# Sixteen pipeline steps instead of four in the body of a loop that five engines run

## The chip, the cores and the metric

The kernel runs on one core of a Trainium2 chip, as one launch. The metric is the device time of that launch in microseconds (us); lower is better. A core has five engines, each with an instruction stream of its own: TensorE (PE; its weight loads are shown apart as PEld), VectorE (DVE), ScalarE (ACT), GpSimd (POOL) and SyncE (SP), which here only issues DMAs. They meet at semaphores.

## The reference

Four batches of 1024 tokens with 128 features. First an attention block with a residual and a layer norm, then six local layers on its result, then one more residual and layer norm. The local layers are nearly all of the work:

```
for i in range(DEPTH):                       # 6 layers
    x = attn_layer(shift_tokens(x), Wqkv[i], q_scale[i], k_scale[i], Wo[i]) + x
    x = ffn_layer(shift_tokens(x), ln_g[i], ln_b[i], W1[i], b1[i], W2[i], b2[i]) + x

attn_layer: q, k, v = split(x @ Wqkv)        # 16 heads of 64
            q, k = l2norm(q) * qs, l2norm(k) * ks, both rotated by tables of position
            softmax over windows of 32 queries against 64 keys, times v, then @ Wo
ffn_layer:  layer norm, @ W1 -> a, gate (341 each);  (a * gelu(gate)) @ W2
```

## The kernel before

`build` makes four parts that follow each other, with all engines meeting between them: `clear_first_rows`, `mla_attention` (the first block; it has a loop of its own over batches, which is not touched), `local_layers`, and `closing_norm`.

`local_layers` cuts a layer into 16 pairs of token tiles (4 batches of 4 pairs, 256 tokens each). The six layers are thus 96 pairs, and the engines run 96 steps plus three that drain the pipeline. A step works on four pairs at different stages: it projects q, k and v for pair t, does scores, softmax and the product with v for pair t-1, the output projection for pair t-2 and the feed-forward part for pair t-3. Each engine's order in a step is written out by hand, and every step has the same order. Four steps (`POS`) are one batch of one layer, which the code calls a round; there are 24 rounds (`ROUNDS`), so 6 layers of 4 rounds.

Every engine's program is made by `rounds(eng, step_fn)`: the first round is written out, with numbers in its semaphore waits, then a hardware loop over rounds 1 to 23 has one round of four steps as its body, with the waits' values worked out in registers from the loop's counter, and then come the three draining steps. In the loop the Python objects `Step` and `Pair` turn the counter into those values, `s.p` is the step's place in its round (0 to 3), and what happens only at some places (SP reloads the projection weights at `s.p == 3`; VectorE and GpSimd clear their link semaphore there) is decided when the program is made. These weights are reloaded in every round, also where the layer stays the same.

On TensorE a step is, in this order: transposes of q and k (L457) with projections (L411) between them, the scores (L468 and L476, two halves for each of two groups of windows), the transpose of the normed x (L498), the product with Wo (L490, `times_wo`), the feed-forward matmuls (L510) among transposes of the probabilities (L421) and projections of v (L411), the transpose of the next x (L397), the product with v in two halves (L433 and L443, `times_v`) around early projections for the next pair (L411), the last feed-forward matmul (L518), one more projection (L411) and the transpose of its result (L498). ScalarE copies each PSUM bank out and frees it; L628 copies the next x once in a step, and L644 the transposed q and k.

Of the kernel before, what the change touches and what calls it, by code (L numbers as in the profile page):

```python
# [22 lines left out]
BATCH, SEQ, DIM = 4, 1024, 128  # L23
# [3 lines left out]
DEPTH, HEADS, DH, WINDOW = 6, 16, 64, 32  # L27
# [5 lines left out]
POS = SEQ // PAIR  # L33
ROUNDS = DEPTH * BATCH
# [100 lines left out]
def local_layers(nc, x_dram, x1_dram, w):  # L135
# [5 lines left out]
    with ExitStack() as ctx:  # L141
# [96 lines left out]
        def rounds(eng, step_fn, last_fn=None):  # L238

            for p in range(POS):
                step_fn(Step(0, p))
            with eng.Fori(1, ROUNDS) as f:
                for p in range(POS):
                    step_fn(Step(f, p))
            for t in range(PAIRS, PAIRS + MAX_LAG):
                step_fn(Step(ROUNDS, t - PAIRS))

# [27 lines left out]
        def _(sp):  # L276
# [40 lines left out]
            def step(s):  # L317
# [47 lines left out]
                if runs(back3):  # L365
# [3 lines left out]
                    if s.p == 2 and in_rounds(s):  # L369

                        load_ffn(s.f)

            rounds(sp, step)
            sp.wait_ge(x2_out, 16 * PAIRS)

        @block.tensor
        def _(pe):
# [148 lines left out]
            def step(s):  # L527
# [60 lines left out]
                if runs(back3):  # L588
                    pe.wait_ge(a_free, ring_a.at(s, "y2T")[1] + 1)
                    transpose_pair(s, "y2", lambda a: y2T[:, P * a:P * (a + 1)])  # L590

            rounds(pe, step)

        @block.scalar
        def _(act):
# [128 lines left out]
            for i in range(EARLY):  # L725
                square(Step(-1, POS - 1).pair(-1), i)
            rounds(act, step)

# [1022 lines left out]
```

## Time and profile before

| what | value |
|---|---|
| median of 3 runs (lowest, highest) | 4710.56 us (4701.91, 4711.07) |
| profiled execution: its own time | 4716.59 us |
| its span, first to last instruction | 4714.8 us |
| PE / PEld busy | 4147.4 (88%) / 2777.6 (59%) us |
| DVE / ACT / POOL busy | 2916.1 (62%) / 2622.4 (56%) / 2799.6 (59%) us |
| mean granted TensorE clock | 0.957 |
| instruction packets: queue q8, queue q14 | 581 (9.52 MB), 147 (1.20 MB) |

The span has three stages: up to about 915 us the first attention block, to about 4680 us the 99 steps of the local layers, then the closing norm. Busy time is the union of an engine's instructions; idle time is put down to what ended it ("<-").
### The profile page before, as it was taken

The page shows a single profiled execution, that of the slowest core. Times are in us where ns is not written, and L with a number is a line of the kernel's source. Part 1 is how long each engine was busy: PE and PEld are TensorE (multiplying, and loading weights), DVE is VectorE, ACT ScalarE, POOL GpSimd, SP SyncE. Part 2 cuts the span into 40 slices and gives each one's busy share as a digit, 9 for nine tenths or more (in the row PEclk, how much of TensorE's full clock was granted, in tenths as well). Part 3 has the DMA queues.
Part 4 walks back from the last instruction along what each step waited for, and adds up shares of the span by engine and source line. Part 5 has one row for each costly group of instructions (what it writes and reads, how often), then busy time and mean ns, then how long its engine had stood idle before and what let it go on. Part 6 is the DMA issues. An engine that isn't in the chain of part 4 may idle for free. (4 is left out here: it accounts for less than half of the span.)

```text
span 4714.8 us, 163642 instructions
## 1 busy us (share of the span) xinstructions
PE 4147.4 (88%) x67078; PEld 2777.6 (59%) x67078; DVE 2916.1 (62%) x4217; ACT 2622.4 (56%) x4417; POOL 2799.6 (59%) x3584
## 2 busy tenths in 40 slices
PE   5878788689999999999999999999999999999994
PEld 2434344356666666666666666666666666666663
DVE  5565656566666666666666666666666666666664
ACT  2535354446556565665656655656566555665662
POOL 0000000177777777777777777777777777777771
PEclk9979788899999999999999999999999999999997
DMA  0000000112222122222222222222222222222223
GB/s 27 3 15 2 16 16 3 42 45 58 69 71 72 51 69 65 72 57 64 65 69 64 56 66 69 77 53 69 65 72 56 65 65 69 64 56 65 69 66 79
DMA packets 284548, 258.85 MB, mean 55 GB/s; under 512 B 122872, under 2 KB 258509, under 8 KB 271149
## 3 DMA queue, kind: packets, MB, share of 16 engines
q1 hardware_dynamic: 283820, 248.14, 19.7%
q8 instruction: 581, 9.52, 0.9%
q14 instruction: 147, 1.20, 0.1%
HBM read 117.63 MB, written 29.77 MB: 31 GB/s over the span
## 5 line engine op out<-in xcount | busy, mean ns | idle before, releaser
L785 DVE TENSOR_TENSOR products<-bank_d,table 128x1024 f32<-128x1024 f32 x772 | 938.1, 1216 | 716.5 <-ACT sq L612 711.8
L908 POOL TENSOR_TENSOR products<-products 128x2048 f32<-128x2048 f32 x192 | 870.4, 4533 | 263.1 <-DVE products L785 263.1
L411 PE MATMUL bank_d<-w_qkv,xT 128*128 128x512 f32 x1544 | 805.6, 625 | 25.2 <-DVE products L785 14.2
L612 ACT ACTIVATE sq<-bank_d 128x512 f32<-128x512 f32 x772 | 467.8, 606 | 484.8 <-PE bank_d L411 474.6
L945 POOL TENSOR_TENSOR qk_rot<-products,rnorm 128x2048 f32<-128x2048 f32 x192 | 695.4, 3622 | 15.0 <-POOL rnorm L927 14.6
L783 DVE TENSOR_REDUCE ss<-sq 128x16 f32<-128x1024 f32 x386 | 468.7, 1214 | 240.3 <-ACT sq L612 240.3
L952 POOL TENSOR_TENSOR prob<-prob,inv_sum 128x1024 f32<-128x1024 f32 x192 | 365.1, 1902 | 407.3 <-DVE inv_sum L765 407.3
L872 POOL MEMSET ident<- 128x128 f32 x1 | 0.2, 204 | 914.6 <-POOLq L1062 914.6
L1489 DVE TENSOR_REDUCE part_max<-s_max 128x1 f32<-128x512 f32 (+3 forms) x768 | 398.3, 554 | 150.7 <-PE s_max L1238 101.2
L457 PE MATMUL bank_a<-ident,qk_rot 128*128 128x128 f32 x3072 | 412.6, 290 | 69.6 <-issue 64.0
L457 PEld LDWEIGHTS bank_a<-ident,qk_rot 128*128 128x128 f32 x3072 | 366.9, 149 | 150.4 <-issue 103.0
L411 PE MATMUL bank_a<-w_qkv,xT 128*128 128x512 f32 x768 | 403.0, 607 | 43.7 <-ACT gate L667 40.5
L1410 ACT ACTIVATE a_probT<-s_T 128x1024 f32<-128x1024 f32 x320 | 299.1, 938 | 249.0 <-PE s_T L1253 152.1
L476 PE MATMUL scores<-kT,qT 64*32 64x64 f32 x24576 | 427.5, 218 | 8.9 <-issue 8.9
L476 PEld LDWEIGHTS scores<-kT,qT 64*32 64x32 f32 x24576 | 362.8, 107 | 99.9 <-issue 99.0
L659 ACT ACTIVATE attnT<-bank_a 128x512 f32<-128x512 f32 x384 | 208.5, 595 | 341.7 <-PE bank_a L443 341.7
L443 PE MATMUL bank_a<-probT,v_back 64*64 64x32 f32 x12288 | 380.2, 221 | 0.0
L443 PE MATMUL bank_a<-probT,v 64*64 64x32 f32 x12288 | 376.6, 220 | 2.6 <-issue 2.1
L648 ACT ACTIVATE prob<-prob 128x1024 f32<-128x1024 f32 x192 | 203.0, 1057 | 284.8 <-DVE prob L755 283.8
L443 PEld LDWEIGHTS bank_a<-probT,v_back 64*64 64x64 f32 x12288 | 332.6, 135 | 42.2 <-issue 40.8
L764 DVE TENSOR_REDUCE row_sum<-prob 128x16 f32<-128x1024 f32 x192 | 233.2, 1215 | 197.7 <-ACT prob L648 197.7
L490 PE MATMUL bank_a<-attnT,w_o 128*128 128x256 f32 x1536 | 350.9, 382 | 1.5 <-issue 1.5
(168 smaller groups left out, 7551.9 us busy)
## 6 DMA issues: line engine op xcount, KB each, us to landing
v_back<-v SPq DMA_DIRECT2D x96, 768.0 KB, 5.5
w_qkv<-in_Wqkv_dram SPq DMA_DIRECT2D x25, 1024.0 KB, 5.0
v_back<-v SPq DMA_DIRECT2D x192, 128.0 KB, 5.5
w_qkv<-in_Wqkv_dram SPq DMA_DIRECT2D x25, 512.0 KB, 5.5
xs<-x_layers SPq DMA_DIRECT2D x194, 64.0 KB, 2.1
w_o<-in_Wo_dram SPq DMA_DIRECT2D x24, 512.0 KB, 6.0
xr<-x_layers SPq DMA_DIRECT2D x96, 128.0 KB, 2.2
x<-x SPq DMA_DIRECT2D x96, 128.0 KB, 1.8
```

The lines of the kernel that those rows point to most:

```text
L411: nc.tensor.matmul(bank[:, :], xT[:, P * a:P * (a + 1)], w_qkv[:, col:col + 512], start=True, stop=True).then_inc(d_filled if i < 8 else a ...
L443: last = nc.tensor.matmul(banks[u][64 * h2:64 * h2 + 64, col:col + 32], src[64 * u:64 * u + 64, a, DH * h:DH * (h + 1)], probT[ph][64 * u: ...
L457: last = nc.tensor.transpose(bank[:, P * j:P * (j + 1)], qk_rot[:, a, col:col + P], ident[:, :])
L476: last = nc.tensor.matmul(scores[row:row + 32, hp, u, :], qT[64 * h2:64 * h2 + 64, hp, 32 * win:32 * win + 32], kT[pair.par][64 * h2:64 * ...
L490: last = nc.tensor.matmul(bank[:, 0:PAIR], w_o[:, hp, :], attnT[:, hp, :], start=(hp == 0), stop=(hp == HP - 1))
L612: nc.scalar.activation(sq[j % 2][:, 8 * c:8 * c + 8, :], bank_d[slot][:, :].rearrange("p (h d) -> p h d", d=DH), ACT.Square).then_inc(squa ...
L783: nc.vector.tensor_reduce(ss[:, a, HEADS * kq:HEADS * (kq + 1)], sq[i // 2 % 2][:, :, :], AX.X, ALU.add)
L785: nc.vector.tensor_tensor(products[:, a, head:head + 8, :, :].rearrange("p h r (o d) -> p h r o d", o=2), bank[:, :].rearrange("p (h r d) ...
L908: link(nc.gpsimd.tensor_tensor(products[:, a, :, 0, :], products[:, a, :, 0, :], products[:, a, :, 1, :], ALU.add))
L945: nc.gpsimd.tensor_tensor(qk_rot[:, a, :].rearrange("p (h d) -> p h d", d=DH), products[:, a, :, 0, :], rnorm[:, a, 0:2 * HEADS].unsqueeze ...
L952: nc.gpsimd.tensor_tensor(prob[ph][:, :, :], prob[ph][:, :, :], inv_sum[:, ph, :].unsqueeze(2).to_broadcast([P, HEADS, 2 * WINDOW]), ALU.m ...
L1489: nc.vector.tensor_reduce(part_max[:, head, col:col + 1], s_max[m % 2][:, 0:width], AX.X, ALU.max).then_inc(max_free, 1)
```

## The change

`rounds` writes out the first four rounds (one layer, 16 steps) instead of one, and its loop runs over layers 1 to 5 with the 16 steps of a layer as its body. The steps themselves, their order, the waits, the DMAs and the draining steps are what they were. In the loop a wait's value is now worked out from the layer's counter.

```
         def rounds(eng, step_fn, last_fn=None):
-            for p in range(POS):
-                step_fn(Step(0, p))
-            with eng.Fori(1, ROUNDS) as f:
+            for b in range(BATCH):
                 for p in range(POS):
-                    step_fn(Step(f, p))
+                    step_fn(Step(b, p))
+            with eng.Fori(1, DEPTH) as layer:
+                for b in range(BATCH):
+                    for p in range(POS):
+                        step_fn(Step(BATCH * layer + b, p))
             for t in range(PAIRS, PAIRS + MAX_LAG):
                 step_fn(Step(ROUNDS, t - PAIRS))
```

The changed file has two lines more, so a line number above 243 is larger by two in it. TensorE before, at the end of the loop's body: the last projection and transpose of a round, the branch, and behind the loop the first matmuls of the draining steps.

```order
L518 MATMUL bank_a<-gate,w 128x256 x3
L382 REGISTER_ALU
L411 MATMUL bank_d<-w_qkv,xT 128x512
L589 REGISTER_ALU
L382 REGISTER_ALU
L498 MATMUL bank_d<-ident,y2T 128x128 x2
L243 REGISTER_ALU
L243 COMPARE_AND_BRANCH
```

TensorE of the changed kernel at the end of a round that is inside the new body: the next round's first transposes (L459) follow with no branch between.

```order
L520 MATMUL bank_a<-gate,w 128x256 x3
L384 REGISTER_ALU
L413 MATMUL bank_d<-w_qkv,xT 128x512
L591 REGISTER_ALU
L384 REGISTER_ALU
L500 MATMUL bank_d<-ident,y2T 128x128 x2
L455 ISA
L391 ISA
L459 MATMUL bank_a<-ident,qk_rot 128x128 x4
```

The branch is gone from three of four round ends inside the body; it stays, as `L244 COMPARE_AND_BRANCH`, at the end of a layer.

TensorE of the changed kernel at the end of the first round (written out): here before stood `L243 UNCONDITIONAL_BRANCH`, the entry into the loop, and then the loop's first transposes with a `REGISTER_ALU` ahead of each group of four.

```order
L520 MATMUL bank_a<-gate,w 128x256 x3
L413 MATMUL bank_d<-w_qkv,xT 128x512
L500 MATMUL bank_d<-ident,y2T 128x128 x2
L459 MATMUL bank_a<-ident,qk_rot 128x128 x16
L413 MATMUL bank_d<-w_qkv,xT 128x512
L459 MATMUL bank_a<-ident,qk_rot 128x128 x16
L413 MATMUL bank_d<-w_qkv,xT 128x512
L470 MATMUL scores<-mask,ident_b 128x512
```

## Rows read from the trace of the kernel before

**Rows 1.** The page, busy time and slices

```profile
PE 4147.4 (88%) x67078; PEld 2777.6 (59%) x67078; DVE 2916.1 (62%) x4217; ACT 2622.4 (56%) x4417; POOL 2799.6 (59%) x3584
PEclk9979788899999999999999999999999999999997
```

**Rows 2.** Waits of PEld from 1071 to 4604 us: total, times, longest us

```profile
PEld scores L468 <- ACT kT L644: 102.7, 92, 1.1
...
PEld bank_a L457 <- issue: 100.4, 121, 3.8
...
PEld bank_a L411 <- ACT gate L667: 78.8, 92, 1.0
...
PEld bank_a L421 <- ACT yT L694: 49.5, 62, 0.8
...
PEld bank_a L490 <- issue: 32.1, 23, 1.6
...
PEld bank_d L411 <- DVE products L785: 14.3, 11, 1.9
```

**Rows 3.** Timeline of ACT, start and length in us, the copy L628

```profile
1064.14 0.38 ACT L628 ACTIVATE xT<-bank_a 128x256 f32<-128x256 f32 x1
...
1101.59 0.38 ACT L628 ACTIVATE xT<-bank_a 128x256 f32<-128x256 f32 x1
...
1138.40 0.38 ACT L628 ACTIVATE xT<-bank_a 128x256 f32<-128x256 f32 x1
...
1175.19 0.38 ACT L628 ACTIVATE xT<-bank_a 128x256 f32<-128x256 f32 x1
...
1212.49 0.38 ACT L628 ACTIVATE xT<-bank_a 128x256 f32<-128x256 f32 x1
...
1255.47 0.38 ACT L628 ACTIVATE xT<-bank_a 128x256 f32<-128x256 f32 x1
...
4594.50 0.38 ACT L628 ACTIVATE xT<-bank_a 128x256 f32<-128x256 f32 x1
```

**Rows 4.** Line 243 (the loop) by engine: ns min/median/max, first and last start

```profile
L243 PEldq COMPARE_BRANCH  x23: 83/3665/3896, 1222.1 to 4603.9; - x23
...
L243 DVEq COMPARE_BRANCH  x23: 50/56/74, 1224.0 to 4605.4; - x23
...
L243 POOLq COMPARE_BRANCH  x23: 40/45/45, 1217.9 to 4599.9; - x23
```

**Rows 5.** Timeline of PE at a taken branch (1376.9) and the last (4603.9)

```profile
1376.53 1.77 PE L411 MATMUL bank_d<-w_qkv,xT 128*128 128x512 f32 x2 [1.91 <-issue]
...
1380.97 2.39 PE L457 MATMUL bank_a<-ident,qk_rot 128*128 128x128 f32 x10 [2.24 <-issue]
...
4603.28 1.12 PE L411 MATMUL bank_d<-w_qkv,xT 128*128 128x512 f32 x2 [0.18 <-issue]
...
4604.46 1.73 PE L457 MATMUL bank_a<-ident,qk_rot 128*128 128x128 f32 x14
```

**Rows 6.** Windows: length, busy PE PEld DVE ACT POOL, clock, DMA, GB/s

```profile
1376.87:1383.70 6.83, 4.59 (x17) 3.19 (x16) 3.33 (x7) 1.79 (x3) 2.30 (x1) 0.50 0.09 27
1383.70:1393.80 10.10, 9.77 (x162) 5.81 (x160) 6.19 (x6) 5.67 (x12) 7.00 (x18) 1.00 0.19 41
```

**Rows 7.** DMA queues from 1226 to 1376 us: packets, MB, share

```profile
q8 instruction: 21, 0.34, 1.0%
q14 instruction: 4, 0.03, 0.1%
```

**Rows 8.** Timeline of PE in the round written out and step 4

```profile
1033.52 0.19 PE L443 MATMUL bank_a<-probT,v 64*64 64x32 f32 x1 [1.92 <-issue]
...
1054.08 2.10 PE L490 MATMUL bank_a<-attnT,w_o 128*128 128x256 f32 x9 [1.49 <-issue]
...
1089.69 0.27 PE L498 MATMUL bank_a<-ident,xn 128*128 128x128 f32 x1 [1.21 <-issue]
```

## The prediction

> **What bounds the kernel now.** I read the page first. TensorE is busy 88% of the span, the next engine 62%, and its granted clock is at 2.4 GHz nearly throughout [rows 1]. The chain that ended last covers only the closing norm, so it does not speak of the loop; the step's length does. ScalarE copies the next x once in a step (L628), so the distance of two such copies is one step [rows 3]: 36.81, 36.79 and 37.30 us, and then 42.98 us, from 1212.49 to 1255.47. That long one holds the loop's branch. The trace has 91 steps from 1101.59 to 4594.50, 3492.91 us in all, with 22 taken branches. If the others take 36.97 (the mean of the three), 129 us are left, 5.9 us for each branch; if they take 36.8, 144 us or 6.5 us. I take **6.2 us for a taken branch**. From 1064.14 to 1101.59 the program passes from the round that is written out into the loop, without a branch and with the same reload of weights, and that step takes 37.45. So the end of a round is not dear; the jump is.
>
> Where do the 6.2 us lie? TensorE's branch instruction takes 3.7 us in the median and 83 ns the one time that it isn't taken [rows 4]. In the shown round TensorE then sits idle 2.24 us ahead of L457; at the last, untaken branch it doesn't [rows 5]. The clock adds to it: 0.50 (1.2 GHz) for 6.83 us around the branch, 1.00 after it [rows 6]. The branch of the other engines takes 45 to 74 ns, and they wait for TensorE meanwhile. A part of the 6.2 us is not the jump: the projection L411 just ahead of it is late too, by 1.91 us in the shown round and 0.18 in the last [rows 5]. I put that at 0.9 us on average, and the jump itself with its slow clock at 5.3.
>
> What is this L411 waiting for? Code arrives in packets of 16 KB, 21 in a time just short of a round [rows 7], for a body of 5,248 instructions: a block is about 256 of them. The two stalls for "issue" in the first round [rows 8] are 768 instructions apart in the program, three blocks exactly, and the third of these rows (1.21 us) five blocks further on. So a **border** between blocks can cost 1 to 2 us where TensorE eats instructions fast (scores, product with v: 256 in about 2 us), since the next block isn't asked for in time. Of some 20 borders in a round most cost nothing. L490 pays in each round (23 times, 32.1 us in all) [rows 2], but two waits behind it, for ScalarE's yT (0.8) and gate (1.0) [rows 2], get shorter by nearly as much: that stall is almost free. A stall between the transpose of the next x and the scores would be paid in full, for there TensorE waits for nothing else.
>
> **The change, part by part.**
>
> *Branches.* 22 taken ones become 4 (five iterations): 18 fewer. With the whole 6.2 us that is 111.6 us. Three round ends of each layer and the three in the first layer turn into plain steps.
>
> *The four that stay.* POOL's body grows from 180 to 714 instructions, VectorE's from 220 to 871, SP's from 97 to 369, so each of them may now have to fetch at the jump as well. POOL's branch of 45 ns [rows 4] may become as long as TensorE's 3.7 us. It comes some 4 us before TensorE's (1217.9 against 1222.1 in the first) and is covered by TensorE's own stall of the same length; without that cover the late one would be qk_rot, at 3.7 us each, 15 us in all. I take 0.
>
> *Borders in the loop.* Before, the body had the same borders in every round, so only the same few places could be unlucky. A step of 1,312 instructions is five blocks and 32 instructions, so over 16 steps the borders drift and pass through every position twice. Placing them by the known stalls (one must lie at L490 of the first step of the old loop and one at its last L411), two in each new iteration fall on the end of the dense product with v or the first L518 behind it, where I expect 2.3 to 2.8 us, paid in full; one falls between the halves of that product, 0.5 to 1.4; two fall on L490, nearly free; the rest on places that cost about nothing in the rows. That makes some 6.5 us per iteration, 32 for five. It takes the place of the 0.9 that each of 22 old round ends paid. Bounds: none at all, and below twice this.
>
> *Borders in the first layer.* A step that is written out has 1,280 instructions, five blocks exactly, so in each of the 12 new steps a border stands in L490 as in the second of [rows 8] (1.49). The two waits behind it give back about 1.3; left are about 0.3 us, 4 in all. If nothing is given back, it is 18.
>
> *Register instructions* of the 12 steps: gone, 32 in a TensorE step. They lie beside running matmuls; plain steps at entry and in the loop differ by less than 1 us. I take 0; if each saved 30 ns it would be 12 us less.
>
> *Sum.* Old excess 22 x 6.2 = 136. New: 4 x 5.3 = 21 for jumps, 32 for borders in the loop, 4 in the first layer, together 57. Gain 79 us. The profiled execution took 4716.6 us, so it would take 4637.6; the median of the runs shown lies 6.0 below it, which gives **4631 us**.
>
> The Trainium skill, "Runtime: NRT & Kernel Launch", section on instruction fetch mechanics, says that the next 16 KiB block (256 instructions) is fetched while the present one runs, that crossing a border is mostly hidden, and that a taken branch out of the window forces a fetch. The trace agrees on the branch (3.7 us) and on most borders, not on all (1.49 and 1.92 us). By the page's rule alone the gain would be the 111.6 us of the branches and no border would cost anything.
>
> **The rivals.**
>
> *Full gain.* Borders cost as little in the new body as in most of the old one, the late L411 vanishes with the branch behind it. For it: only one place in a round of some 20 borders pays regularly, and it is nearly free. Against: the 1.92 in the product with v [rows 8]. 4716.6 - 111.6 - 6.0 = 4599 us. This is what the Trainium skill's rule in the page named above gives.
>
> *Borders bite harder.* Each iteration has four full stalls of 2.5 us instead of two and a half, and two of them pull the clock down as the jump does [rows 6], worth 1.7 more each (of the jump's 5.3, what its 3.7 doesn't explain): 5 x (4 x 2.5 + 2 x 1.7) = 67. The first layer pays 9, half of its bound. With 21 for the jumps that is 97, the gain 39 and the time 4671 us.
>
> *Slower.* One mechanism: asking for the next block late, at most borders. TensorE crosses five borders in each of the 92 steps concerned; the gain of 111.6 is gone when a step loses 1.2 us on average, one border in five at 1.2 us, fully paid. At one in three at 1.25 us (2.1 us a step) the time is 4710.6 - 111.6 + 193 = 4792 us. Against: the plain steps at 36.8 with five borders each [rows 3].
>
> *No change.* The long step is due to the round's end (weights, ScalarE) and not to the jump; then it stays, and the time is 4711 us. Against: 83 ns and no idle time at the untaken branch [rows 4, 5], and 37.45 at the entry [rows 3].
>
> **How the numbers follow.** A measurement of this kernel tells about 0.2% (9.4 us) from no change. Chances: forecast 0.50 (4612 to 4650), full gain 0.25 (4590 to 4612), borders bite harder 0.16 (4650 to 4700), slower 0.05, no change 0.04. The first three are all faster by over 0.2%: so faster 0.91, same 0.04, slower 0.05. The range reaches from a little below the full gain (an excess of 6.5 us instead of 6.2 gives 117 us, 4594) to where harder borders are mostly taken in, 4668.
>
> **What the profile after would show.** TensorE's COMPARE_BRANCH 5 times, four at 3.3 to 3.9 us and one short. Distances of L628 copies of 36.8 to 37.5 at three of four round ends, 42 to 44 at four places only. The clock at 0.50 in the loop four times instead of 22. "issue" ahead of L457 down from 100.4 by about 60 us. New "issue" gaps of 2 to 3 us ahead of L518 or L411 behind the product with v, once in eight steps and always at the same steps; if they are missing, the full gain is right. L490 late in each of the first layer's steps, L421 and L411 waiting less. Wrong would be: round ends that stay at 43 us without a branch, a POOL or VectorE branch of microseconds that TensorE waits for, or plain steps above 38 us throughout.

## The result and the profile after

| | before | after |
|---|---|---|
| median of 4 runs each | 4709.5 us (4701.9 to 4711.1) | 4761.8 us (4757.3 to 4761.9) |
| ratio after / before | | 1.0112, 95% interval 1.0097 to 1.0127 |
| profiled execution | 4716.6 us | 4761.9 us, span 4760.1 |

The changed kernel is **1.1% slower**; 4631 us, 1.7% faster, was predicted. I read its profile in the order of the prediction. The page first: busy time per engine, granted clock in slices, and the queues that carry code (packets, MB).

```profile
PE 4164.5 (87%) x67078; PEld 2787.4 (59%) x67078; DVE 2916.3 (61%) x4217; ACT 2618.1 (55%) x4417; POOL 2805.6 (59%) x3584
PEclk9979888899999999999999999999999999999997
...
q8 instruction: 554, 9.08, 0.8%
q14 instruction: 214, 1.75, 0.1%
```

Nothing there tells where the 52 us between the medians (45.3 between the two profiled executions) went: against [rows 1] TensorE is busy 17 us longer, and the clock's tenths are the same but for one slice. The branches (L244, formerly L243) went as forecast, five times, and none of another engine is long:

```profile
L244 POOLq COMPARE_BRANCH  x5: 40/45/50, 2137.0 to 4645.0; - x5
L244 PEldq COMPARE_BRANCH  x5: 83/3608/3820, 2141.1 to 4648.9; - x5
```

The timeline of ScalarE's copy of the next x, now L630, tells it. The one that ends the first round is at 1065.56 and the 92nd after it at 4639.52, 3574.0 us, against 3530.4 (from 1064.14 to 4594.50) in [rows 3]: 43.6 of the 45.3 us lie in these 92 steps. Round ends without a branch take 36.7 to 37.6 us in the loop, as forecast (one in the first layer takes 38.5). But in each sixteen, steps in the middle are long:

```profile
1693.30 0.38 ACT L630 ACTIVATE xT<-bank_a 128x256 f32<-128x256 f32 x1
...
1735.86 0.38 ACT L630 ACTIVATE xT<-bank_a 128x256 f32<-128x256 f32 x1
...
1780.45 0.38 ACT L630 ACTIVATE xT<-bank_a 128x256 f32<-128x256 f32 x1
...
1817.25 0.38 ACT L630 ACTIVATE xT<-bank_a 128x256 f32<-128x256 f32 x1
...
2006.81 0.38 ACT L630 ACTIVATE xT<-bank_a 128x256 f32<-128x256 f32 x1
...
2048.25 0.38 ACT L630 ACTIVATE xT<-bank_a 128x256 f32<-128x256 f32 x1
...
2093.77 0.38 ACT L630 ACTIVATE xT<-bank_a 128x256 f32<-128x256 f32 x1
```

42.56, 44.59, then 36.80 again; later 41.44 and 45.52. The steps of an iteration are counted from 0, the one that holds the loop's entry or its branch. In the first of the five iterations steps 5, 6, 11, 13 and 14 are such (step 11, not shown, takes 42.4), in the others the same ones, with step 13 between 38.9 and 41.7. The waits of the weight load for "issue" (total, times, longest, us), from 1055 to 4642 us after, and from 1071 to 4604 us before:

```profile
PEld scores L478 <- issue: 118.0, 386, 4.2
PEld bank_a L445 <- issue: 109.5, 122, 5.6
...
PEld bank_a L520 <- issue: 57.9, 165, 3.8
...
PEld bank_a L459 <- issue: 46.7, 112, 4.0
...
PEld bank_a L492 <- issue: 7.9, 9, 1.2
```

```profile
PEld scores L476 <- issue: 95.1, 378, 1.6
...
PEld bank_a L518 <- issue: 44.5, 186, 0.2
...
PEld bank_a L443 <- issue: 39.8, 96, 0.4
```

The jump's wait (L459, before L457) fell from 100.4 [rows 2] to 46.7. The waits of the product with v (L445) grew by 70 us, with single waits of up to 5.6 us; the longest before was 0.4. One of them, in the timeline of TensorE and the windows around it (length, busy PE PEld DVE ACT POOL, clock, DMA share, GB/s):

```profile
1742.16 0.29 PE L445 MATMUL bank_a<-probT,v 64*64 64x32 f32 x6
1747.11 0.31 PE L445 MATMUL bank_a<-probT,v 64*64 64x32 f32 x1 [4.66 <-issue]
```

```profile
1739.00:1742.30 3.30, 3.30 (x115) 2.16 (x113) 1.80 (x2) 2.06 (x4) 2.64 (x8) 1.00 0.90 254
...
1744.84:1751.66 6.82, 4.55 (x25) 3.10 (x26) 1.04 (x1) 1.68 (x3) 1.28 (x2) 0.50 0.09 20
```

A stall of 4.66 us in the middle of a product, and 6.8 us at half the clock (1.2 GHz) that begin 2.3 us before the stall ends. And the DMA engines are 90% busy up to the moment at which TensorE runs dry. The DMA view of 1744.5 to 1745.5 us holds the code packet that ends the stall:

```profile
q1 hardware_dynamic: 65, 0.16, 74.7%
q8 instruction: 1, 0.02, 8.0%
```

From 1739.0 to 1744.5 there is none; it starts at 1744.6, 2.3 us after TensorE ran dry. The late packet I saw at once; the DMA share beside it I read past at first, as the order of the experiments shows.

### The profile page after: what moved, and what is told of

Same layout as the page of the kernel before. It is cut to its first block and busy times, and to the rows that moved or that the text cites. A ratio compares the mean times of both kernels' runs of the same rounds, so it can differ in the third digit from the quotient of the medians.

```text
span 4760.1 us, 162061 instructions
## 1 busy us (share of the span) xinstructions
PE 4164.5 (87%) x67078; PEld 2787.4 (59%) x67078; DVE 2916.3 (61%) x4217; ACT 2618.1 (55%) x4417; POOL 2805.6 (59%) x3584
## 5 line engine op out<-in xcount | busy, mean ns | idle before, releaser
L413 PE MATMUL bank_d<-w_qkv,xT 128*128 128x512 f32 x1544 | 817.1, 633 | 6.2 <-DVE products L787 4.8
L445 PE MATMUL bank_a<-probT,v 64*64 64x32 f32 x12288 | 385.4, 220 | 45.8 <-issue 45.5
L459 PE MATMUL bank_a<-ident,qk_rot 128*128 128x128 f32 x3072 | 390.1, 280 | 20.9 <-issue 14.6
L445 PE MATMUL bank_a<-probT,v_back 64*64 64x32 f32 x12288 | 386.1, 221 | 24.3 <-issue 24.3
L459 PEld LDWEIGHTS bank_a<-ident,qk_rot 128*128 128x128 f32 x3072 | 347.7, 143 | 94.1 <-issue 49.9
L445 PEld LDWEIGHTS bank_a<-probT,v_back 64*64 64x64 f32 x12288 | 335.5, 135 | 69.3 <-issue 67.2
L445 PEld LDWEIGHTS bank_a<-probT,v 64*64 64x64 f32 x12288 | 339.7, 136 | 47.9 <-issue 47.9
```

The lines of the kernel that those rows point to most:

```text
L413: nc.tensor.matmul(bank[:, :], xT[:, P * a:P * (a + 1)], w_qkv[:, col:col + 512], start=True, stop=True).then_inc(d_filled if i < 8 else a ...
L445: last = nc.tensor.matmul(banks[u][64 * h2:64 * h2 + 64, col:col + 32], src[64 * u:64 * u + 64, a, DH * h:DH * (h + 1)], probT[ph][64 * u: ...
L459: last = nc.tensor.transpose(bank[:, P * j:P * (j + 1)], qk_rot[:, a, col:col + P], ident[:, :])
```

## The experiments

Each time is the median of its runs; ratios are to the kernel before on the same chip (4702 to 4712 us). Step times are distances of ScalarE's copy as above. "Theory 1" is the prediction's own, made harsher: a border between code blocks is dear wherever TensorE eats instructions fast.

### Which engine's body costs

TensorE alone gets the body of sixteen, and then all engines but TensorE:

```diff
-            rounds(pe, step)
+            rounds(pe, step, long_body=True)   # other engines: round of four
```

> Only TensorE has the written-out layer and the body of sixteen steps; the other four engines keep the round of four. Theory 1 (borders between TensorE's code blocks): the time is that of the changed kernel, 4762 us within 10, and the slow steps stand at the same places (steps 5, 6, 11, 13 and 14 of each sixteen). Theory 2 (the longer streams of the other engines, whose code packets rose from 147 to 214): clearly below, between 4600 (the gain of 18 branches undisturbed) and 4709.

Measured: 4797.2 us (ratio 1.019, 1.016 to 1.022), its profiled execution 4762.6, the fastest of four that reach up to 4810.5. Each round's end inside the body now takes 38.9, though TensorE doesn't jump there: 18 times 2.1 us is 38, about what the time lies above the 4762 expected (35). Steps 5, 11, 13 and 14 are long again, with the product with v waiting up to 5.6 us at once. But step 6 is long (44.0) in one iteration of the profiled execution only and takes 37.2 to 38.0 in the other four, where the changed kernel has 44 to 45 in all five. TensorE's program is the same in both, so its borders alone do not make this stall.

> The opposite: ScalarE, VectorE, GpSimd and SyncE have the body of sixteen steps, TensorE keeps its round of four. Theory 1: as before, 4709 us within 10. Theory 2: the loss of the changed kernel shows, 4762 us or more, since TensorE keeps its 22 taken branches as well.

Measured: 4707.6 us (0.999, 0.998 to 1.000); round ends at 43. So the loss comes with TensorE's longer code and not with the others', and the round ends of the run before suggest that the other engines' jumps are worth 2.1 us a round where TensorE's own jump doesn't cover them (tested further on).

### Moving all borders

Two kernels were to shift TensorE's code by 128 no-operations. The no-operations were dropped when the program was built, so these are the two kernels of the case once more and say nothing on the theory:

> The kernel before with 128 no-ops on TensorE ahead of its first wait in the local layers, where it idles 22 us anyway; nothing else changes but where the borders between blocks of 256 instructions fall. Theory 1: each of the 23 rounds gets the borders of steps 5 to 8 of the changed kernel's sixteen (42.6, 44.6, 36.8, 36.9 us, 161 in all) and keeps its taken branch (5.3): 166 instead of 153.7 us a round, 23 times, so about 4990 us. Theory 2, or borders that cost little: 4709 to 4716 us.

> The changed kernel with the same 128 no-ops. A step moves the borders by 32 instructions, so 128 are four steps. Theory 1: the slow steps of each iteration move to four places earlier, 1, 2, 7, 9 and 10 instead of 5, 6, 11, 13 and 14; the five iterations take the same within 15 us in all. In the first layer (1,280 instructions a step, borders at fixed places) all borders move by 128, which may cost anything from nothing to 8 us a step: 4762 to 4860 us. Theory 2: the slow steps stay where they are.

Measured: 4708.7 us (0.999, 0.997 to 1.000) and 4766.5 us (1.013, 1.010 to 1.015), a repeat of the result.

What does shift the borders is to place the head of TensorE's loop at a chosen slot of a block of 256. In the kernel before it stands at about 138:

```diff
-            with eng.Fori(1, ROUNDS) as f:
+            loop = nc.Fori(1, ROUNDS, engines=OrderedEngineSet([eng.engine]), head_slot={eng.engine: 10})
+            with loop as f:
```

> The kernel before, with the head of TensorE's loop laid on slot 10 of a block of 256 instructions, where it stands at about slot 138 now. Nothing else changes. Theory 1 (borders): each round gets the borders of steps 5 to 8 of the changed kernel's sixteen (42.6, 44.6, 36.8, 36.9 us) and its taken branch (5.3): 166 instead of 153.7 us a round, about 4990 us. Theory 2 (the losses of the changed kernel come from something else, borders cost little): 4700 to 4720 us.

Measured: **4983.8 us (1.060, 1.054 to 1.065)**. Same instructions, same branches in the loop, 6% slower, within 10 us of what was expected: the first round in the loop reads 43.4, 44.7, 37.1, 42.6. The borders' places matter more here (274 us) than all branches together (about 145).

> The same with the head on slot 66, so that the four steps get the borders of the changed kernel's steps 7 to 10, which took 36.7 to 36.9 us nearly always. Theory 1: the late last projection of a round (0.9 us) goes, the taken branches stay: 0.9 x 22 = 20 us less than before, 4690 us. Theory 2: 4700 to 4720 us.

Measured: 4788.6 us (1.018, 1.016 to 1.020). Missed by 100 us: in the fourth step of 22 of the 23 rounds TensorE waits 3.0 to 4.1 us at a border in the scores, although step 10 of the changed kernel, which has its borders at the same places, took 36.7. Carrying step times over from the changed kernel named the dear places at slot 10 and failed here, so the place of a border does not by itself give its price.

### Announcing the branch

Rival (the announced branch does not help, only the place of borders matters): 4700 to 4710. Second rival (some border stalls by 3.5 us a round as with slot 66): 4700 or more, one step of each round at 40 to 41.

> The same as the run with slot 106, and the back branches of the other engines' loops announced too (their heads stay where they are). If the 39 us that remain at each round's end are the other engines' jumps (2.1 us a round by the run in which PE alone had no branch), the round end falls from 39.1 to 37 to 38: 4570 to 4600 us. Rival: the others' branches stand too near a block's beginning for the announcement to help, or their blocks are hidden anyway: the same as slot 106 alone, within 0.2%.

Measured: 4718.1 us (1.002, 1.000 to 1.003); 4745.2 (1.008, 1.005 to 1.010); 4723.0 (1.005, 1.003 to 1.007); 4694.6 (0.998, 0.997 to 1.000). Expected were 4620, 4600, 4613 and 4570 to 4600: all four missed, the first because the announcement does nothing at the old place, the others because of stalls at borders that are left. TensorE's branch in the first two, by line (the 24th in the second is the entry into the placed loop):

```profile
L248 PEldq COMPARE_BRANCH  x23: 88/3666/3866, 1216.6 to 4606.9; - x23
```

```profile
L248 PEldq COMPARE_BRANCH  x24: 87/456/1487, 1070.0 to 4633.1; - x24
```

With the hint at the old place, where the branch stands some 10 instructions behind a border (138 + 5,248 is 21 blocks and 10), it still takes 3.7 us; where it stands 190 or more behind one, 0.5 us. At slot 66 the hint takes round ends from 42.4 to 39.2; with all engines announced, at slot 106, they are 37.7. The 3.2 us a round that the hint saves at slot 66 would make 70 us; the third and fourth steps give back 1.3 us a round of it, and the time falls by 43. Slot 106 ran into a border in the scores again, and not in each round:

```profile
PEld scores L481 <- issue: 178.6, 415, 4.1
```

The same border, some 565 instructions into the fourth step, stalled by 3.4 to 3.9 us in 16 of 23 rounds and not at all in the other seven. Nothing in TensorE's own program differs between them, so theory 1 falls here. Nor does the DMA traffic ahead of it tell them apart. In windows at the same place of the step (2 us around the beginning of the scores; a round with the stall, then one without; clock, DMA share and GB/s at the end) it is nearly the same, and so it is in all but two of the 23 rounds (0.74 to 0.87; the two, without the stall, have 0.55 and 0.64):

```profile
1948.10:1950.10 2.00, 1.71 (x33) 0.66 (x36) 0.81 (x2) 1.69 (x5) 2.00 (x1) 1.00 0.85 223
1648.80:1650.80 2.00, 1.71 (x33) 0.66 (x35) 0.81 (x2) 1.72 (x5) 2.00 (x1) 1.00 0.82 235
```

What differs is when TensorE's code packets start, counted from the first matmul of the scores (L481). In the seven rounds without the stall one starts 3.4 to 0.9 us ahead of it and the next 2.9 to 3.3 us behind it. In the sixteen with the stall the first starts from 0.7 us ahead to 1.1 us behind, and the next only when TensorE has run dry. The DMA queues from 1.5 to 8 us behind it, in the round without the stall (1651.9 to 1658.4 us) and in the one with it (1951.2 to 1957.7 us), where no line of q8 stands:

```profile
q1 hardware_dynamic: 969, 1.07, 52.7%
q8 instruction: 1, 0.02, 1.2%
```

```profile
q1 hardware_dynamic: 874, 0.67, 37.6%
```

So a packet that comes a little late is followed by one that comes far too late. Step 11 of the changed kernel is also a fourth step of a round, and the traffic at these places is SP's reload of the projection weights (1024 KB), which only the fourth step has. No run changes that reload.

### TensorE written out

With no loop and no register arithmetic on TensorE a step is about five whole blocks:

```diff
+                for f in range(1, ROUNDS):         # TensorE only
+                    for p in range(POS):
+                        step_fn(Step(np.int64(f), p))
```

> Only PE's program is written out in full for all 24 rounds, with no loop and no register arithmetic; the other engines have the round of four. A step is then 1,280 instructions or five whole blocks, as in the first layer, so the borders stay where they are from step to step and never wander. Theory 1: no step of 41 us or more; round ends at 38.9 from the other engines' jumps, 36.8 x 3 + 38.9 = 149.3 us a round, about 4610 us. Rival (the long code by itself is slower, wherever its borders lie, since its blocks are never fetched twice): steps of 41 to 45 as in the changed kernel, 4700 or more.

Measured: 4674.2 us (0.994, 0.992 to 0.996). The expected 4610 was missed by 64 us. For two thirds of the span the rounds read about as expected (36.9, 36.8, 36.9, 38.9, with two ends of 40.6 and 40.8). Then single steps of 40 to 43.7 appear. All TensorE's code is fetched once and never again, and the kernel is still faster than before, so length by itself isn't dear. The borders do wander, against the expectation: in the built program every second pair of steps has 1,279 instructions instead of 1,280 each, 46 fewer over 92 steps, which moves the borders later in the step, towards the end of the product with v. The next three vary the others' programs only:

> PE's program written out in full, the other engines with the changed kernel's body of sixteen steps. If the remaining 2.1 us of each round's end are the other engines' jumps, 18 of 23 round ends fall from 38.9 to 36.9: 38 us less than with PE written out alone (4674), so 4636 us. Rival (the 38.9 are PE's own or come from elsewhere): 4674, round ends at 38.9. The slow steps of the last third (41 to 43 us) should stay at about the same steps if PE's borders alone make them, as the borders stand where they stood; if the others' fetches decide, they move.

> PE's program written out in full, the other engines with the round of four and their back branches announced at the top of the body. Announcing them with PE's loop in place took round ends from 39.1 to 37.7. The same here: 38.9 to 37.6, 23 x 1.3 = 30 us less than with PE written out alone, 4644 us. Rival (the gain there was a side effect of where PE's borders fell): 4674.

> PE's program written out in full, the other engines with the body of sixteen and their back branches announced. Expected 4630 us: what the body of sixteen gives (4636) and 5 x 1.3 us for the five jumps that are left. Rival (the longer code of the others costs elsewhere): not below the run with the round of four and announced branches.

Measured: 4634.5 us (0.985, 0.983 to 0.986), 4627.0 (0.983, 0.981 to 0.985), 4617.6 (0.981, 0.980 to 0.983). Expected were 4636, 4644 and 4630; the second and third came out 17 and 12 us better. Up to the last third round ends fall to 36.7 to 37.4 in both ways (with sixteen steps but for the one in sixteen that still has a jump, 39.1), so the 2.1 us were the others' jumps. The steps of 40 to 43 us stay in the last third but only in part at the same steps. Borders alone would have left them in place: something beside TensorE's code decides.

### The copies into v_back

The changed kernel's loop has 25 stalls of over 2 us besides those at the branch, five in each iteration. In 24 of them the DMA share is 0.67 or more in the 4.6 us around the moment at which TensorE's weight load runs dry (0.50 in the other); at the four taken branches it is 0.28 to 0.37. Around the product with v and the L520 behind it most of the bytes are copies of v into v_back, 1 MB a step, which SP issues when v has been evicted; the product with v of the pair before runs meanwhile. **Theory 3**: the code packet waits behind them. The test leaves 15/16 of their bytes out from the fourth step on, so its result is not the reference's, and keeps every instruction:

```diff
+                    w = INNER if isinstance(s.t, int) and s.t < 3 else 64
-                    sp.dma_start(dst[q:P, :, :], src[0:P - q, :, :]).then_inc(done, 16)
+                    sp.dma_start(dst[q:P, :, 0:w], src[0:P - q, :, 0:w]).then_inc(done, 16)
...
```

> The changed kernel, in which the copies into v_back carry only 64 of 1,024 columns from the fourth step on, so the local layers compute with old values of v_back; every engine's program is otherwise the same and the block borders stand where they stood. Theory 3 (the code packet waits behind the copies' packets): the stalls of 3 to 5 us ahead of L445, L520 and L478 (here one line later) shrink to under 1.5 us, the sixteen steps have 37 to 38.5 in place of 41 to 45.5, about 25 us less per iteration and 4640 us in all; only the stall at the branch stays. Theory 1 (a border is dear where TensorE eats instructions fast, whatever the DMA engines do): the same stalls, 4750 to 4762 us.

> The kernel before with the same lighter copies, the control for what the copies cost there. Theory 3: only the small stalls ahead of L490 and L411 can shrink, the branch's 43 us steps stay: 4680 to 4710 us, so that the body of sixteen steps is then the faster one by 1 to 1.5%. Theory 1: 4709 within 0.2%, and the body of sixteen still 1.1% slower.

Measured: **4641.8 us (0.988, 0.984 to 0.991)** for the changed kernel and 4705.9 (1.001, 0.999 to 1.002) for the kernel before. The same border in the first slow step, in TensorE's timeline of the changed kernel and then with light copies:

```profile
1703.32 0.30 PE L445 MATMUL bank_a<-probT,v 64*64 64x32 f32 x3 [3.78 <-issue]
```

```profile
1704.43 0.30 PE L446 MATMUL bank_a<-probT,v 64*64 64x32 f32 x3 [0.76 <-issue]
```

The 5 us ahead of the moment at which TensorE runs dry, in both (DMA share 0.70 and 0.20):

```profile
1694.40:1699.40 5.00, 5.00 (x216) 3.82 (x209) 2.04 (x2) 2.22 (x4) 3.83 (x14) 1.00 0.70 177
```

```profile
1698.60:1703.60 5.00, 5.00 (x210) 3.77 (x203) 2.12 (x2) 2.22 (x4) 3.83 (x14) 1.00 0.20 43
```

Waits with light copies, 1518 to 4640 us:

```profile
PEld scores L479 <- issue: 84.2, 332, 3.9
...
PEld bank_a L446 <- issue: 55.3, 104, 1.8
...
PEld bank_a L460 <- issue: 40.6, 91, 4.3
```

The product with v never waits longer than 1.8 us. The jump's stall (L460) stays, and the kernel before keeps its time: light copies don't make branches cheaper. With them the body of sixteen is the faster one, 64 us or 1.4% below the control. The stalls are smaller but not gone: steps 6 and 14 still take 37.5 to 41.0, not the 37 to 38.5 expected. The stall in the scores (step 11) is left in one iteration of five, although the weights' reload that stands beside it is the same; in the other four one code packet starts 14.4 to 14.6 us behind the step's copy of x and the next at 18.1 to 18.4, in the changed kernel at 16.1 to 16.6 and 25.4 to 26.0.

Is it the traffic or the depth of the queue? All bytes are moved again, the large copy in four slices, each issued when the one before has landed:

```diff
-                    sp.dma_start(dst[q:P, :, :], src[0:P - q, :, :]).then_inc(done, 16)
+                    for c in range(4):
+                        lo, hi = INNER // 4 * c, INNER // 4 * (c + 1)
+                        if c:
+                            sp.wait_ge(done, 96 * now.k + 16 * c)
+                        sp.dma_start(dst[q:P, :, lo:hi], src[0:P - q, :, lo:hi]).then_inc(done, 16)
+                    sp.wait_ge(done, 96 * now.k + 64)
```

> The changed kernel with the large copy into v_back (768 KB a step) cut into four slices of 256 columns, each issued when the one before has landed; all bytes are moved. If the code packet waits behind what is already queued, it now finds at most a quarter in front of it: the stalls of 3 to 5 us ahead of L445 and L520 shrink to 1 to 2 us, and the time lies nearer to that with light copies (4642) than to that of the changed kernel (4762): about 4670 us, faster than the kernel before. Rival (the total traffic counts, or the slices keep the queues busy longer and meet more borders): 4740 to 4790 us.

> TensorE's program written out in full, the other engines with the body of sixteen and announced branches (4618 us), and the copies into v_back in the same four slices. The slow steps of the last third (39 to 43 us) come from borders in the product with v beside those copies and should go to 37 to 38: 15 to 25 us less, about 4598 us. Rival (the slices hold up SP's other issues, so that x or the weights come late): 4618 or more.

Measured: **4661.9 us (0.990, 0.988 to 0.992)** and **4606.2 us (0.979, 0.977 to 0.982)**. The first is the changed kernel with all its work, 100 us faster by slicing one copy. The same border again, and the waits of 1518 to 4640 us:

```profile
1700.48 0.30 PE L450 MATMUL bank_a<-probT,v 64*64 64x32 f32 x3 [0.77 <-issue]
```

```profile
PEld scores L483 <- issue: 95.8, 339, 4.4
...
PEld bank_a L450 <- issue: 61.0, 103, 2.9
```

The 5 us ahead of the moment at which TensorE runs dry there:

```profile
1694.70:1699.70 5.00, 5.00 (x207) 3.72 (x201) 2.17 (x2) 2.22 (x4) 3.83 (x14) 1.00 0.34 87
```

So the total of the bytes does not decide; how they are issued does. Whether it is the depth of the queue isn't separated: slicing also spread the traffic, and the DMA share ahead of this border is 0.34 instead of 0.70. Step 14 (41.0 to 43.7 us; 38.8 to 41.0 with light copies) and, from the third iteration on, step 6 (40 to 42) are still long. The second, TensorE written out, the others with sixteen steps and announced branches, and sliced copies, is the fastest kernel of this study (4598 was expected); its steps of 40 us and more in the last third are gone.

## Why the prediction was wrong

**The branches**: right. Old excess over 36.8 us a step was 3530.4 - 92 x 36.8 = 145 us (I had 136). The four that stay cost 26 us (steps of 42.3 to 43.8) where I had 21. Eighteen fewer are worth about 118 us (an estimate, 18/22 of 145), 111.6 predicted.

**No cost at the other engines' bodies**: right with TensorE's jump in front of them; their branches still take 45 to 63 ns. Without that cover they cost 2.1 us a round, which the prediction looked for in POOL's branch and priced at 3.7.

**Borders in the first layer, 4 us**: right. From 1065.56 to 1508.22 twelve steps take 442.7 us, 1 us over 12 x 36.8.

**Borders in the loop, 32 us**: this step failed. The excess there is 3574.0 - 92 x 36.8 - 26 - 1 = 161 us, 32 us for each iteration where I had 6.5 and twice that as the upper bound. The sum then is 26 + 1 + 161 = 188 against 145: 43 us slower, where the profiled executions differ by 45.3 (the medians by 52, since the profiled execution before was 7 us above its median). The mechanism, code that comes late at a border, was named rightly and its places partly (the product with v, L520 behind it; not the scores of step 11), but two things were wrong in it. First the price of one: I read 1.2 to 1.9 us from four stalls of the kernel before [rows 5, 8] and took 2.3 to 2.8 for the worst. In the first iteration they are 3.9, 4.8, 4.2, 3.5 and 3.1 us, 19.5 in all, and the five steps exceed 36.8 by 32.5; the 13 us between fit what half the clock can cost in the 27 us that it was granted there (an estimate: at most 13.7). In the forecast I had put the clock only at the jump. Second the reason: "where TensorE eats instructions fast" gave me two and a half places per iteration. Four of the five dear places, in steps 5, 6, 13 and 14, are where the copies into v_back are in the DMA queues, which meet the end of the product with v in each step; the fifth, in step 11, stands beside the reload of the projection weights. With 15/16 of the copies' bytes left out the excess of the 92 steps over 36.8 us falls from 188 to 72 us. In the loop of the kernel before the product with v never waited longer than 0.4 us. But two of my four stalls were beside the same copies, the 1.91 us ahead of L411 and the 1.92 in the written-out round, and I had not looked at the DMA share ahead of them. The 3.3 us before each (clock, DMA share and GB/s at the end):

```profile
1371.30:1374.60 3.30, 3.30 (x76) 2.30 (x68) 2.87 (x4) 1.62 (x3) 3.30 (x1) 1.00 0.96 226
1028.30:1031.60 3.30, 3.30 (x91) 2.01 (x84) 1.15 (x2) 2.22 (x4) 2.47 (x11) 1.00 0.91 228
```

So the rows named the neighbour, but as a price they were too low: beside the same copies the stalls in the changed kernel's loop are 2.5 to 5.6 us. *Slower* was the rival that came true, with a chance of 0.05, although by five dear borders in sixteen steps and not by most borders.

The Trainium skill, "Runtime: NRT & Kernel Launch", section on instruction fetch mechanics, has each engine fetch its next block over a DMA queue of its own and calls a crossing mostly hidden. The first half agrees with the trace (q8, 554 packets) and held the clue; the second doesn't here: up to 5.6 us where the copies are under way, 1.8 at most in the product with v where they are light.

*Shown*: that the loss comes with TensorE's longer code and not with the other engines'; that places decide by up to 6%; that the copies into v_back make borders in the product with v dear, and that the way they are issued decides, not their total. *Argued only*: that the packet waits inside the DMA engines (the trace shows when it starts, not when it was asked for), and that the depth of the queue is what counts and not the rate of the traffic, as the slices changed both. *Open*: the dear border in the scores (16 of 23 rounds at slot 106). The traces show that the packet before it comes later in those rounds, but not why, nor why the next one then isn't there. Open too is what stays long in step 14 with sliced copies.

## What to carry to other kernels

Code comes over the DMA engines too. Before a loop's body grows past what repeats at fixed places, look at what the DMA engines do where its borders will fall, and keep large copies in short slices when a busy engine needs its next block meanwhile. A body whose length is a whole number of blocks keeps its borders still; one with 32 instructions more visits each bad place in turn. And before you take a stall's length from a row as a price, look at what else was busy beside it.

## What was unexpected on the hardware

- The same instructions with the loop's head at another slot of a block: 4709 to 4984 us.
- A code packet that takes 1.3 us starts up to 2.8 us after TensorE ran dry; the whole stall is up to 5.6 us. In 23 of the 25 stalls of over 2 us in the changed kernel's loop a stretch of 3.4 or 6.8 us at 1.2 GHz begins 1.5 to 5.1 us after TensorE's weight load ran dry.
- An announced branch takes 0.5 us instead of 3.7, but only where it stands far behind a border: 190 instructions did, 10 did not.
- The copies, 1 MB a step, kept the DMA engines 90% busy for 3.3 us; with the large one in four slices the stall at the same border went from 3.78 to 0.77 us, as much as with 1/16 of the bytes (0.76).
- At one border of one program, 16 rounds of 23 have a stall of 3.4 to 3.9 us and seven have none. In the sixteen the code packet before comes up to 4.5 us later, and the next some 7 us later than in the seven.
